# Flamingo block on one core: a ternary sum, LayerNorm steps and the last refinement put elsewhere

## The reference

```python
x = x + tanh(g_xattn[0]) * xattn0(layernorm(x), ctx)             # 16 heads of 16, 77 keys
x = x + tanh(g_ffn[0])   * ffn0(layernorm(x))                    # ternary weights, 8-bit rounding
x = x + tanh(g_xattn[1]) * xattn1(layernorm(x), ctx, distances)  # bias -|s| * log(distance)
x = x + tanh(g_ffn[1])   * ffn1(layernorm(x))                    # expert 0, then its own layernorm
```

## Time and profile before

| | |
|---|---|
| median of 3 runs | 401.23 us (400.35 to 402.42) |
| profiled execution | 401.5 us, its span 399.8 us |
| mean granted PE clock | 0.94 of 2.4 GHz |
| busy: PE, DVE, ACT, POOL | 83%, 70%, 71%, 58% of the span |
| attention 0, slots 0 to 3 | about 16 to 66 us |

### The profile page before, as it was taken

How to read it: one execution, slowest core, us unless ns; L and a number is a source line. 1 busy time by engine, 2 the same in 40 slices (tenths; PEclk the granted TensorE clock), 3 DMA queues, 4 the chain that set the end, 5 groups by cost and what they waited for, 6 DMA issues and landing times.

```text
span 399.8 us, 8924 instructions
## 1 busy us (share of the span) xinstructions
PE 330.6 (83%) x3222; PEld 271.1 (68%) x3222; DVE 278.8 (70%) x676; ACT 283.1 (71%) x516; POOL 231.0 (58%) x413
## 2 busy tenths in 40 slices
PE   2877978878886774878787899899898799999993
PEld 2555767766764542456556688788687699888882
DVE  5888556776787657989955557777847548666665
ACT  4474796899896777999934798866679757555540
POOL 2577634786477322458794755566785257544444
PEclk9986779999699869889999999999999999999998
DMA  7796552311100000320092222211200000000001
GB/s 215 171 132 148 149 134 87 73 41 43 43 3 21 2 0 2 51 27 2 2 260 52 51 53 53 52 31 24 53 2 2 2 0 30 28 28 27 28 28 52
DMA packets 23187, 22.02 MB, mean 55 GB/s; under 512 B 4711, under 2 KB 22504, under 8 KB 23067
## 3 DMA queue, kind: packets, MB, share of 16 engines
q1 hardware_dynamic: 23144, 21.45, 22.1%
HBM read 10.34 MB, written 2.10 MB: 31 GB/s over the span
## 4 chain that ended last, share of the span: by engine, by line
PE 46%; DVE 19%; ACT 19%; issue 10%; POOL 3%; DMA 1%; SPq 0%; ACTq 0%; POOLq 0%; DVEq 0%
PE psA L1744 10%; PE psA L1521 6%; PE psBE L1728 5%; PE psD L1728 4%; PE psD L1430 3%; ACT pp_hi L736 3%; DVE mx L1139 3%; PE psBE L1456 2%; DVE ham L1187 2%; DVE st L896 2%; PE psA L1505 2%; ACT p L727 2%; PE psA L1697 2%; ACT xn L700 2%; PE psA L1345 2%
## 5 line engine op out<-in xcount | busy, mean ns | idle before, releaser
L510 POOL TENSOR_TENSOR pp_lo<-p,pp_hi 124x512 f16<-124x512 f32 x80 | 92.8, 1179 | 45.6 <-ACT pp_hi L736 45.5
L1139 DVE TENSOR_REDUCE mx<-psBE 128x6 f32<-128x462 f32 (+1 forms) x96 | 54.9, 582 | 36.4 <-PE psBE L1456 36.1
L406 POOL TENSOR_TENSOR lns<-lns,mhalf 128x2 f32<-128x2 f32 x39 | 31.1, 796 | 83.2 <-DVE lns L901 82.8
L727 ACT ACTIVATE p<-psD 124x512 f32<-124x512 f32 x80 | 47.7, 597 | 30.2 <-PE psD L1430 29.3
L1430 PE MATMUL psD<-qb,ktb 98*124 98x256 f16 (+1 forms) x256 | 50.1, 294 | 4.5 <-DMA qb<-mT 3.9
L736 ACT ACTIVATE pp_hi<-p 124x512 f16<-124x512 f32 x80 | 50.4, 630 | 0.0
L1430 PEld LDWEIGHTS psD<-qb,ktb 98*124 98x124 f16 (+1 forms) x256 | 33.7, 147 | 8.5 <-DMA qb<-mT 5.0
L1456 PE MATMUL psBE<-kt_hi,q_hi 128*128 128x154 f16 (+2 forms) x160 | 34.9, 288 | 3.1 <-ACT mT L718 2.2
L1744 PE MATMUL psA<-ew_hi,pp_lo 128*128 128x256 f16 x128 | 34.9, 273 | 0.0
L1744 PE MATMUL psA<-ew_hi,pp_hi 128*128 128x256 f16 x128 | 34.9, 273 | 0.0
L1744 PE MATMUL psA<-ew_lo,pp_hi 128*128 128x256 f16 x128 | 34.9, 273 | 0.0
(11 more groups left out here) (210 smaller groups left out, 993.7 us busy)
## 6 DMA issues: line engine op xcount, KB each, us to landing
qb<-q_hi SPq DMA_DIRECT2D x32, 128.0 KB
xs<-in_x SPq DMA_DIRECT2D x8, 256.0 KB, 5.3
qb<-q_lo SPq DMA_DIRECT2D x16, 128.0 KB
tw_raw<-in_tw SPq DMA_DIRECT2D x2, 1024.0 KB, 5.8
space<-in_ew SPq DMA_DIRECT2D x2, 1024.0 KB, 6.8
out<-space SPq DMA_DIRECT2D x7, 256.0 KB, 2.1
ktb<-km SPq DMA_DIRECT2D x6, 248.0 KB, 5.6
qb<-bT_lo SPq DMA_DIRECT2D x8, 104.0 KB
```

The lines of the kernel that those rows point to most:

```text
L510: nc.gpsimd.tensor_tensor(pl[:, u % 2, 2 * r:2 * r + 2, :], p32[:, n % 4, :, :], ph[:, u % 2, 2 * r:2 * r + 2, :], ALU.subtract).then_inc( ...
L727: a_(p32[:, n % 4, :, :], psD[n % 2][0:KR, :].rearrange("p (t r) -> p t r", t=2), ACT.Exp, scale=1.0 / SSC).then_inc(a["exp"], 1)
L1139: v.tensor_reduce(pairs[:, MP[k][0]:MP[k][1]:MP[k][2], :], psBE[:, n % 2, 0:hn * KEYS].rearrange("p (q e k) -> p q e k", e=2, k=KEYS), AX. ...
```

## The change

The ternary sum of the first weights goes on ACT from the end of slot 2 to slot 3, step 3, ahead of that step's exponent. The transposes of sub-block 7 go on PE from slot 3, step 0, to step 1, their copy on ACT from step 1 to step 2. On DVE the statistics of sub-blocks 6 and 7 go from slot 1, steps 3 and 5, to slot 1, step 5, and slot 2, step 1, and the key rows from slot 0, step 4, to step 5; within a step the steps of LayerNorm come behind the maximum. On POOL the factors of sub-block 6 go from the middle of slot 1 to the start of slot 2, those of 7 from the start of slot 2 to behind its subtraction (0, 4). In the last half-blocks POOL keeps the power, and the four refining steps go to DVE.

```diff
@@ POOL: factors_half
                 nc.gpsimd.tensor_tensor(g[:, 1, :], g[:, 0, :], mhalf[:, 0:1], ALU.pow).then_inc(s_rs, 1)
-                pool.wait_ge(s_rs, n + 1 + j)
-                link(nc.gpsimd.tensor_tensor(g[:, 2, :], g[:, 1, :], g[:, 1, :], ALU.mult))
-                link(nc.gpsimd.tensor_tensor(g[:, 3, :], g[:, 0, :], g[:, 2, :], ALU.mult))
-                link(nc.gpsimd.tensor_scalar(g[:, 4, :], g[:, 3, :], -0.5, 1.5, ALU.mult, ALU.add))
-                nc.gpsimd.tensor_tensor(g[:, 5, :], g[:, 4, :], g[:, 1, :], ALU.mult).then_inc(E["fac"], 1)
@@ POOL: attn_slot and the loop over slots
-                    if l == 0 and s == 1 and r == 1:
-                        factors_act(6, SX, L0["fac"])
+                    if l == 0 and s == 2 and u == 1 and r == 0:
+                        factors_act(7, SX, L0["fac"])
                     plo(l, u, r)
...
-                    factors_act((4, 5, 7)[s], SX, L0["fac"])
+                    factors_act(4 + s, SX, L0["fac"])
@@ ACT: setup, attn_slot
-                if (s, r) in ((1, 4), (2, 4), (3, 1)):
+                if (s, r) in ((1, 4), (2, 4), (3, 2)):
                     ln0_transposed(2 * s + 1)
...
+                if s == 3 and r == 3:
+                    ternary_sum(0)
...
-                if l == 0 and s in (2, 3):
-                    ternary_sum(s - 2)
+                if l == 0 and s == 3:
+                    ternary_sum(1)
@@ DVE: ln0_steps
-                if (s, r) in ((0, 0), (0, 2), (0, 5), (1, 1), (1, 3), (1, 5)):
-                    ln0_stats({(0, 0): 2, (0, 2): 3, (0, 5): 4, (1, 1): 5, (1, 3): 6, (1, 5): 7}[s, r])
+                if (s, r) in ((0, 0), (0, 2), (0, 5), (1, 1), (1, 5), (2, 1)):
+                    ln0_stats({(0, 0): 2, (0, 2): 3, (0, 5): 4, (1, 1): 5, (1, 5): 6, (2, 1): 7}[s, r])
...
-                if (s, r) == (0, 4):
+                if (s, r) == (0, 5):
                     key_rows()
@@ DVE: expert_norm_half
+            def expert_factors_half(j):
+                n = 5 * NU - 1
+                g = lns[:, n % 4, :, j:j + 1]
+                dve.wait_ge(s_rs, n + 1 + j)
+                link(v.tensor_tensor(g[:, 2, :], g[:, 1, :], g[:, 1, :], ALU.mult))
+                link(v.tensor_tensor(g[:, 3, :], g[:, 0, :], g[:, 2, :], ALU.mult))
+                link(v.tensor_scalar(g[:, 4, :], g[:, 3, :], -0.5, 1.5, ALU.mult, ALU.add))
+                link(v.tensor_tensor(g[:, 5, :], g[:, 4, :], g[:, 1, :], ALU.mult))
...
-                dve.wait_ge(e["fac"], u + 1 + j)
+                expert_factors_half(j)
@@ PE: attn_slot
-                    if l == 0 and (s, r) in ((1, 3), (2, 3), (3, 0)):
+                    if l == 0 and (s, r) in ((1, 3), (2, 3), (3, 1)):
                         ln0_transposes(2 * s + 1)
```

More of the change, by code:

```diff
@@ L1254, in expert_sum_half @@
                 link(v.bn_aggr(mv[:, n % 4, j, :], st[:, n % 4, j, :]))
-                v.tensor_scalar(lns[:, n % 4, 0, j:j + 1], mv[:, n % 4, j, 1:2], EPS * SY * SY, None,
-                                ALU.add).then_inc(s_var, 1)
+                g = lns[:, n % 4, :, j:j + 1]
+                v.tensor_scalar(g[:, 0, :], mv[:, n % 4, j, 1:2], EPS * SY * SY, None, ALU.add).then_inc(s_var, 1)
+            def expert_factors_half(j):
+                n = 5 * NU - 1
+                g = lns[:, n % 4, :, j:j + 1]
+                dve.wait_ge(s_rs, n + 1 + j)
[3 more added lines that the diff above has]
+                link(v.tensor_tensor(g[:, 5, :], g[:, 4, :], g[:, 1, :], ALU.mult))
             def expert_norm_half(j):
```

## The result

The changed kernel took 396.99 us (median of 9 runs, 396.1 to 398.67) against 401.23 (399.16 to 404.26, 9 runs); the ratio is 0.9894, with a 95% interval from 0.9855 to 0.9934. Timed again in a later series it was 0.9909 (0.9873 to 0.9944). The forecast was 397.6, with a range from 395.4 to 400.6. The profiled execution of it took 398.31 us, span 396.6: it is one of the slower ones, so the spans differ by 3.2 us and the medians by 4.2.

A forecast was written before the change was run, and what follows sets the result against it. In slot 3 ACT and PE were taken to wait for each other in turn, with PE at half clock meanwhile. The terms -3.8 - 0.3 + 0.44 = -3.66 us gave 397.6 us, range 395.4 to 400.6.

The forecast's parts named there:

- The sum and the transposes, -3.8: Slots 2 and 3 of the first attention: slot 3 takes 11.0 us instead of 14.8, 3.8 less.
- PE needs 9.1 and ACT is the bound: Slot 3: at full clock PE needs 9.1 us, ACT's work is 10.82, so ACT bounds it.
- Rival 1: Slot 3 stays at half clock, PE needing 12.1 us: only 2.0 us shorter, time 399.4; chance 0.14.
- rival 4: Slower: ACT late in slot 3, PE idles about 2.5 us, slot 4 gets the low clock; 403.9 us; chance 0.05.
- Statistics, factors and key rows, -0.3: Slots 0 to 2: moving statistics 6 saves 0.3 us (0 to 1.0); key rows and statistics 7 cost nothing.
- rival 3: POOL's late factors 7 hold back LayerNorm 7's application; the 2.47 us stall stays; about 400.0 us; chance 0.05.
- The tail, +0.44: After 391 us: DVE runs both halves' small steps in a row, 0.44 us more (+0.2 to +0.8).
- rival 2: The gain is given back at a later clock fall, 6.4 us at half clock costing 3.05: 400.6 us; chance 0.10.

The follow-up runs named there:

- e1_sum: The kernel before with only the first ternary sum moved to slot 3, step 3; 397.4 us against 400.18, ratio 0.9925.
- e7_nosum: The changed kernel with the first ternary sum cut to 8 columns of each row chunk; slot 3 10.82 us in a single execution.
- e6_awake: The kernel before with PE repeating throwaway products during its wait for LayerNorm 7; 398.02 us against 400.18, ratio 0.9944.
- e2_transposes: The kernel before with only the transposes of LayerNorm 7 and their copy one step later; 400.33 us against 400.18, ratio 1.0001.
- e8_old_stats: The changed kernel with the tail split between POOL and DVE, and statistics, POOL's factors and key rows in the old order; 398.45 us, ratio 0.9964.
- e5_tail_split: The changed kernel with half 0 of the tail refined on POOL and half 1 on DVE; 397.64 us, ratio 0.9931.
- e10_all: The changed kernel with the tail split between POOL and DVE and throwaway PE products in three idle stretches; 397.21 us, ratio 0.9915.
- e12_best: The changed kernel with the tail split between POOL and DVE and throwaway PE products at 133.3 and 164.2 us only; 393.29 us against 400.46, ratio 0.9847.

## Why the prediction was right, and where it wasn't

*The sum and the transposes, -3.8.* Measured -3.87, and `e1_sum` gives the same with the sum alone. The size held; two of its reasons didn't. The step "PE needs 9.1 and ACT is the bound", from which I took 10.82 plus 0.2, is wrong for all but the slot's first 4 us: without the sum on ACT slot 3 keeps its length (`e7_nosum`). PE is busy for 9.38 of 10.85 us and waits, ahead of 55.1, for the shifts, the DMA and ACT's copy; these waits, 1.5 us in all, were missing from my 9.1. That both engines end within 0.6 us of each other made the two bounds give one number. And the transposes' new place, which I took as part of the cure, does nothing beside the sum's, and nothing measurable alone.

*What the stall costs.* I wrote that the clock is low "while it happens" and reckoned it into the sum (6.11 us of work to 3.05). That was the part that matters: 3.01 of 3.87 us by `e6_awake`. Rival 1, half clock all through slot 3, would have left 2.0 us of the gain; the clock held, and no gap of PE there was over 0.78 us. The 2.5 us of idling from which rival 4 was to decide have no support: in `e2_transposes` the clock fell after gaps of 1.94 and 1.35 us.

*Statistics, factors and key rows, -0.3.* The profile pair shows -1.05, just past my bound of 1.0, but nine and five profiles of the two orders show a scatter of 2.4 us and more, and the two timed comparisons differ in sign. The argument for the key rows (what comes sooner at the end of slot 0 is lost in the ping-pong of tables) fits the means of the table above and not the pair `e8_old_stats` and `e5_tail_split`. The term of -0.3 is neither confirmed nor refuted. POOL's factors for LayerNorm 7 were ready when ACT asked: rival 3 didn't come.

*The tail, +0.44.* Measured 0.46, in the place said. The rule of the Trainium skill (Advanced Engine Details and Errata, VectorE Performance Modes) that two-port DVE instructions and GpSimd's block each other would, as the prediction applied it, have made it 0.33 more; DVE's TENSOR_SCALAR at 391.28 ran its 0.15 us while POOL's power ran from 391.04 to 391.60. I applied it wrongly, though: by the conditions in that section a step needs a dimension above one to take a two-port mode, and a step on 128x1 has none. The row that does speak against the rule for POOL's power is that of the earlier trace rows, a TENSOR_SCALAR of 512 columns at its 0.47 us.

*The sum.* -3.87 + 0.46 = -3.41, and with the 1.2 us given back between slot 3 and ternary sub-block 5 the parts that the profiles show come to -2.2. The medians differ by -4.24, with an interval from -2.6 to -5.8 (0.9934 and 0.9855 of 401.23), and in the second timing by -3.3. What makes up the 1 to 2 us between the parts and the medians no experiment shows; slots 0 to 2 scatter by more than that. So the forecast of 397.6 against 396.99 is in part luck: a loss of 1.2 that it left out was made good by something that it didn't name. The sum alone agrees better: -3.87 and what it gives back make some -2.7, and `e1_sum` measured -2.8.

I had a give-back at a later fall as rival 2, at 3.05 us and 0.10. It came beside the forecast's case and not in its place, and smaller: 0.8 us in one slot of the ternary stage, where the low stretch was 6.8 us long instead of 3.4, and up to 0.4 ahead of it. The ternary stage has such falls in every profile of both kernels, and I had thought of them as fixed. They belong in the terms.

## What to carry to other kernels

A wait of TensorE can cost what the clock takes behind it as well as its own length: here a gap of 2.47 us cost 3.87, of which 3.01 went away when PE was given throwaway products in the gap, the wait itself staying. Look for low stretches of the granted clock, go back to the gap ahead of each, and either take the cause away or fill it, with products that need nothing which comes late: in `e10_all` fourteen that waited for a late copy cost 2.3 us. Not every gap does this: with gaps of 0.36 and 0.78 us slot 3 kept its clock at 1.00. In a tail, count the moved steps on the engine that receives them: two engines side by side took 1.77 us here, one that waited for nobody 2.54.

## What was not expected of the hardware

- In the ternary stage most falls come at the same place in the work in profile after profile (read from the granted clock in stretches of half a microsecond). In slots 4 to 7 they don't: there the first one came at 102 us in the kernel before, at 98 in the changed one, at 77 in `e2_transposes` and at 76 in `e12_best`. The slot from sub-block 4 to 5 took 7.2 to 7.3 us in the kernel before and in the two experiments that left slot 3 long (low from 172.8 to 176.2, 174.0 to 177.4 and 175.0 to 178.4), and 8.1 to 8.4 us in all eight profiles with a short slot 3 in which the gap wasn't filled (low from 165.4 to 172.2 in the earliest, 167.7 to 174.5 in the latest). The gap ahead of it was the same, 3.77 us. Why the longer low stretch goes with the shorter slot 3 stays open. The prediction let the place of the falls vary by execution; the two profiles of the changed kernel don't show it: the later one has its falls 0.4 to 1.2 us sooner, about as much as its shifts of slot 0 (23.5 against 24.3).
- A small DVE step on two SBUF inputs can be held up by POOL's large subtraction as well: in the changed kernel a step on 128x1 took 1.12 us and ended when the first of POOL's two subtractions, 53.17 to 54.33, did. Steps of that kind and size take 0.16 at 391.47.

```profile
53.22 1.12 DVE L1021 TENSOR_TENSOR dcol<-dcol,bc 128x1 f32<-128x1 f32 x1
```
